# A four-layer gated network with cross attention on one core: where softmax sums and reciprocals are issued, when x comes back from DRAM, and which small loads stand in blocks of their own

## The reference, cut to what matters

```
q, k, v = proj(x), proj(ctx), proj(ctx)
p = exp(q k^T * scale - row maximum)        # layer 1: clipped to +-50, masked, no maximum
out = (p v) / p.sum(-1)
```

## Time and profile before

| | |
|---|---|
| time, median of 3 runs | 3059.93 us (3059.43 to 3064.61) |
| the profiled execution | 3059.54 us, span 3057.8 us |
| PE busy | 2632.1 us (86%) |
| PEld | 1671.9 us (55%) |
| DVE | 1753.8 us (57%) |
| ACT | 1196.7 us (39%) |
| POOL | 930.9 us (30%) |
| layer 1 attention starts | 549 us (its mask block 546) |
| layer 2 attention | starts 1537 us, first scores 1624.8 us |
| layer 3 attention | starts 2207 us, first scores 2276.8 us |

### The profile page before, as it was taken

How to read it: one execution, slowest core, us unless ns; L and a number is a source line. 1 busy time by engine, 2 the same in 40 slices (tenths; PEclk the granted TensorE clock), 3 DMA queues, 4 the chain that set the end, 5 groups by cost and what they waited for, 6 DMA issues and landing times. The chain is left out here.

```text
span 3057.8 us, 36158 instructions
## 1 busy us (share of the span) xinstructions
PE 2632.1 (86%) x11447; PEld 1671.9 (55%) x11447; DVE 1753.8 (57%) x3263; ACT 1196.7 (39%) x2550; POOL 930.9 (30%) x434
## 2 busy tenths in 40 slices
PE   7998799788887679999959998738699998699898
PEld 3555487655434456656546553426476653477555
DVE  2444576467765989989377664512277773444221
ACT  0222222267743688788014555111125553222111
POOL 0222000066732110010015775033318982322122
PEclk9998899899988889999979999869899999799999
DMA  9663113665403410100063421074465430212722
GB/s 278 223 241 139 55 62 124 182 166 142 111 1 114 165 56 28 46 37 28 14 170 107 132 68 29 1 288 110 106 183 172 121 102 1 84 41 71 262 56 47
DMA packets 137548, 333.52 MB, mean 109 GB/s; under 512 B 18608, under 2 KB 21681, under 8 KB 133041
## 3 DMA queue, kind: packets, MB, share of 16 engines
q1 hardware_dynamic: 110192, 262.71, 27.7%
q0 software_dynamic: 12864, 29.06, 4.1%
q10 hardware_dynamic: 14336, 39.85, 3.9%
HBM read 237.24 MB, written 97.72 MB: 110 GB/s over the span
## 5 line engine op out<-in xcount | busy, mean ns | idle before, releaser
L1982 POOL TENSOR_TENSOR L_attn_total<-L_attn_total,L_attn_probs 128x2048 f32<-128x2048 f32 x103 | 471.8, 4581 | 31.6 <-ACT L_attn_probs L1910 22.1
L2016 DVE TENSOR_REDUCE L_attn_row_max<-L_attn_rows_ps 128x1 f32<-128x512 f32 x512 | 338.9, 684 | 149.6 <-PE L_attn_rows_ps L1776 145.5
L1910 ACT ACTIVATE L_attn_probs<-L_attn_s_ps 128x512 f32<-128x512 f32 x512 | 288.0, 601 | 269.1 <-PE L_attn_s_ps L1797 264.2
L521 PE MATMUL L_ffn_hidden<-L_ffn_x_high,L_ffn_up_high 128*128 128x512 f32 x688 | 295.9, 430 | 73.2 <-DVE L_ffn_routes L432 25.8
L1797 PE MATMUL L_attn_s_ps<-L_attn_q_stack,L_attn_k_stack 98*128 98x512 f32 (+1 forms) x768 | 311.7, 432 | 21.1 <-ACT L_attn_probs L1910 20.7
L398 ACT ACTIVATE L_ffn_sums<-sims 128x128 f32<-128x128 f32 x1024 | 314.5, 389 | 29.0 <-DVE L_ffn_routes L418 22.3
L521 PE MATMUL L_ffn_hidden<-L_ffn_x_low,L_ffn_up_high 128*128 128x512 f32 x688 | 272.8, 397 | 0.0
L1776 PE MATMUL L_attn_rows_ps<-L_attn_k_stack,L_attn_q_stack 96*128 96x512 f32 x512 | 223.1, 439 | 23.0 <-DVE L_attn_row_max L2016 17.1
L542 PE MATMUL L_ffn_y<-L_ffn_down_in,L_ffn_h 128*128 128x512 f32 x512 | 230.8, 596 | 1.9 <-DVE L_ffn_h L649 1.9
L1797 PEld LDWEIGHTS L_attn_s_ps<-L_attn_q_stack,L_attn_k_stack 98*128 98x128 f32 (+1 forms) x768 | 145.7, 194 | 158.1 <-ACT L_attn_probs L1910 73.3
L1910 ACT ACTIVATE L_attn_probs<-L_attn_s_ps,keep_mask 128x512 f32<-128x512 f32 x256 | 183.8, 783 | 82.8 <-DVE L_attn_s_ps L2028 82.4
(11 more groups left out here) (310 smaller groups left out, 4526.2 us busy)
## 6 DMA issues: line engine op xcount, KB each, us to landing
L_attn_k_stack<-k_parts SPq DMA_DIRECT2D x144, 256.0 KB, 4.8
L_attn_q_stack<-q_parts SPq DMA_DIRECT2D x72, 256.0 KB, 6.0
k_parts<-L_attn_stage SPq DMA_DIRECT2D x32, 512.0 KB, 2.8
L_attn_abs_in<-in_L_ffn_w SPq DMA_DIRECT2D x12, 1024.0 KB, 10.8
L_attn_kv_parts<-L_attn_part ACTq DMA_DIRECT2D x12, 1024.0 KB, 4.8
L_attn_ctx<-ctx_parts SPq DMA_DIRECT2D x24, 512.0 KB, 9.3
L_attn_wv<-L_attn_kv_parts SPq DMA_DIRECT2D x24, 512.0 KB, 7.1
q_parts<-L_attn_stage SPq DMA_DIRECT2D x24, 512.0 KB, 3.6
```

Source lines behind the costliest of these rows:

```text
L521: last = nc.tensor.matmul(hidden_ps[0:m, b, side, :], w[:, i, e0:e0 + m], x_parts[xp][:, i, h * HALF:(h + 1) * HALF], start=(q == 0), stop ...
L1910: nc.scalar.activation(probs[:, g % P_SLOTS, h, :], s_ps[:, v % S_SLOTS, :], ACT.Exp, **kinds).then_inc(exp_done, 1)
L1982: nc.gpsimd.tensor_tensor(total[:], first, probs[:, g % P_SLOTS], ALU.add).then_inc(added, 1)
L2016: nc.vector.tensor_reduce(row_max[:, hq, i:i + 1], rows_ps[:, r % R_SLOTS, :], AX_X, ALU.max, negate=True).then_inc(max_done, 1)
```

## The change

- The output weights of layer 0 are loaded into the tiles of its value weights, from SP's list of the block before; its output block waits for nothing of its own.
- `key_mask_block` goes. The attention loads the mask first and VectorE converts it there.
- The biases are loaded ahead of the query weights in all three softmax attentions.
- `ffn_block` sets `tile_stats.taken` again after the work that runs in its beginning, so layer 2's attention uses the statistics taken at the end of layer 1.
- Layer 2's attention: DIRECT 2 for 1, sums at unit 2, reciprocals in eight parts of 64 columns at units 3, 3, 4, 4, 10, 10, 10, 10, and another opening.
- `routed_block` no longer loads x; layer 3's attention does, and takes the statistics at the new word S0 of its own opening. In the other openings S0 is the first word.

```diff
@@ ffn_block
             env.prefix = name
+            env.tile_stats.taken = final
@@ routed_block, sync
                 sp.wait_ge(summed, 16 * I)
-                if not last:
-                    for t in range(TILES):
-                        sp.dma_start(env.x[:, t, :], sums[t * P:(t + 1) * P, :]).then_inc(back[t], 16)
@@ routed_block, vector
                 copy_y(I - 1)
-                if not last:
-                    for t in range(TILES):
-                        dve.wait_ge(back[t], 16)
-                        env.tile_stats.take(env, dve, t)
-                    env.tile_stats.finish(dve)
@@ streamed_attention_block
-    DIRECT = {n: int(made or n == SETS - 2) if less_max_rows else 3 if n == SETS - 2 else 2 for n in range(SETS - 1)}
+    DIRECT = {n: 2 if made else int(n == SETS - 2) if less_max_rows else 3 if n == SETS - 2 else 2 for n in range(SETS - 1)}
...
-    SUMS_AT = 7 if less_max_rows else PV_AT
-    INVERT_AT = {u: part for part, u in enumerate((8, 9, 10, 11) if less_max_rows else (4, 6, 7, 8, 9, 10, 11, 12))}
-    INVERTED = SEQ // len(INVERT_AT)
+    SUMS_AT = 7 if less_max_rows and not made else PV_AT
+    invert_units = (3, 3, 4, 4, 10, 10, 10, 10) if made else (8, 9, 10, 11) if less_max_rows else (4, 6, 7, 8, 9, 10, 11, 12)
+    INVERT_PARTS = len(invert_units)
+    INVERT_AT = {u: [part for part, v in enumerate(invert_units) if v == u] for u in invert_units}
+    INVERTED = SEQ // INVERT_PARTS
...
     if made:
-        order = ("N0 X0 X1 N2 W0 W1 X2 X3 N4 Q00 V00 V01 X4 X5 W2 W3 N6 Q01 V02 V03 X6 X7 Q02 Q03 Q10 Q11 T0 Q12 Q13")
+        order = ("W0 W1 N0 N2 X0 X1 X2 X3 N4 Q00 W2 Q01 W3 V00 Q02 V01 N6 Q03 X4 X5 V02 X6 X7 V03 Q10 Q11 T0 Q12 Q13")
...
     else:
         order = ("N0 N1 K00 N2 N3 X0 X1 K01 N4 N5 X2 X3 W0 W1 V00 N6 N7 X4 X5 Q00 W2 W3 V01 X6 X7 Q01 K10 K11 "
                  "V02 V03 Q02 Q03 Q10 Q11 T0 Q12 Q13")
+    if x_sums is None:
+        order = "S0 " + order
+    else:
+        order = ("K00 K01 V00 V01 V02 S0 N0 N1 V03 X0 X1 W0 W1 N2 N3 X2 X3 Q00 N4 N5 W2 W3 Q01 X4 X5 N6 N7 K10 Q02 X6 X7 K11 "
+                 "Q03 Q10 Q11 T0 Q12 Q13")
@@ streamed_attention_block, sync
+                if not less_max_rows:
+                    sp.dma_start(mask_raw[:], io["mask"]).then_inc(mask_loaded, 16)
+                parts.load_biases(env, sp)
+                if x_sums is not None:
+                    for t in range(TILES):
+                        sp.dma_start(env.x[:, t, :], x_sums[t * P:(t + 1) * P, :]).then_inc(x_back[t], 16)
                 parts.first_loads(env, sp)
@@ streamed_attention_block, vector
+                def statistics():
+                    if not taken_before:
+                        for t in range(TILES):
+                            if x_sums is not None:
+                                dve.wait_ge(x_back[t], 16)
+                            nc.vector.bn_stats(stats[:, t, :], env.x[:, t, :]).then_inc(stats_done, 1)
...
@@ linear_attention_block, sync
+                sp.wait_ge(v_done, CT)
+                sp.dma_start(wv[:], wo_dram).then_inc(env.wo_loaded, 16)
+                sp.dma_start(bv[:], io["bo"].partition_broadcast(P)).then_inc(env.wo_loaded, 16)
```

More of the change, by code:

```diff
@@ L917, in _, with routed_block @@
                 dve.sem_inc(slots.placed, 1)
-def routed_block(env, name, slots, weights, load_weights, E, sums, last, ahead=None):
+def routed_block(env, name, slots, weights, load_weights, E, sums, ahead=None):
     nc = env.nc
@@ L934, in routed_block @@
     kept, summed, weighed = env.sem("kept"), env.sem("summed"), env.sem("weighed")
-    back = [env.sem(f"back{n}") for n in range(TILES)]
     weight_step = env.sem("weight_step")
@@ L1582, in streamed_attention_block @@
     env.wo_loaded = env.sem("wo_loaded")
+    x_back = [env.sem(f"x_back{t}") for t in range(TILES)] if x_sums is not None else []
     with ExitStack() as local:
@@ L1848, in _ @@
                         turn(0)
-                    elif item[0] not in "WN":
+                    elif item[0] not in "WNS":
                         for c in range(DC):
@@ L2521, in sb @@
             return local.enter_context(nc.sbuf_tensor(f"{name}_{n}", shape, dt))
-        if early:
+        if weights:
+            wo, bo = weights
+        elif early:
             wo, out_rows = env.out_weights[:, 0], env.out_weights[:, 1]
@@ L2758, in x_hat, with expert_layer @@
                 yield
-        def expert_layer(name, gate, shared, normalise, sums, last=False, ahead=None):
+        def expert_layer(name, gate, shared, normalise, sums, ahead=None):
             with sublayer() as local:
@@ L2890, in build @@
             expert_layer("L3_ffn", env.tanh_gates[:, 7:8], io["L3_ffn_shared_w1"].shape[0], False,
[L2891 removed]
+                         out.rearrange("b s d -> (b s) d"))
         else:
```

100 lines of the change are left out of this document (47 added, 53 removed).

## The result

The changed kernel took 3076.81 us (median of 5, 3076.05 to 3082.73), the kernel before 3059.93 beside it: ratio 1.0059, 95% interval 1.0045 to 1.0073. Forecast was 3064, +4.8 on the profiled execution; the profiled execution is 16.7 longer (span 3074.5 against 3057.8).

What follows compares the result with a forecast made beforehand. TensorE, busy 2632 of 3058 us, was taken as the bound. Terms -5.3 - 2.9 - 4.8 + 9.8 + 8.0 = +4.8 on the profiled 3059.54 gave 3064 us, range 3047 to 3077.

Steps and rivals of the forecast that it cites:

- C and D: Opening of layer 2's attention: kept statistics and the new order together save time, -4.8 us (-1 to -9).
- E: Layer 2's attention sets: third addend, earlier sums and reciprocals in eight parts cost +9.8 us.
- F: Layer 3's attention: x reloaded inside it and the new opening order cost +8.0 us (-6 to +12).
- A: Layer 0's output block: loading its weights early removes TensorE's wait, -5.3 us (-4.8 to -6.5).
- B: Before layer 1's attention: dropping the mask block and loading biases earlier saves -2.9 us (-2.4 to -3.4).
- Q00 starts at 23, -4.2: Layer 2's opening: first query product starts 23 us after the attention's start, 4.2 us earlier than before.
- about 1 less: Layer 2's opening: TensorE's 4.42 us wait behind N6 shrinks by about 1 us, since GpSimd's subtractions come earlier.
- I take the same loss: Layer 2's sets: slow clock costs as much as before, some 7.9 us over five sets.
- only one half of keys is left beside it, so I take 10.7: Layer 3's opening: first query product's end to first row takes 10.7 us, against 13.2 before.
- With the 1.3 of a block border the attention starts at 2197.35, 9.9 before: Border into layer 3: attention starts 1.3 us after the last sum lands, 9.9 us earlier than before.
- rival B2: Layer 3's opening: TensorE finds no costly hole, the 9.9 us arrive whole, 3046 us; chance 0.15.
- B3: Layer 2's sets: the clock loses more, making them cost +20 us, 3074 us in all; chance 0.20.

Runs made afterwards that it cites:

- best1: Changed kernel with E undone, layer 3's old order, x loads issued at routed block's end, awaited in attention, no GpSimd drain there: 3046.84 us, ratio 0.9959.
- A to D alone: Changed kernel with E and F both undone: 3051.16 us, ratio 0.9978 to the kernel before.
- E_late_inv: Changed kernel with layer 2's reciprocals in four parts of 128 columns at units 8 to 11, sums still at unit 2: 3065.37 us, ratio 1.0027.

## Why the prediction was wrong

The sign of every part was right; the sum was 12 us too low. Of these, 2.1 are in C and D, 0.3 in E, 3.7 in F's border, 1.5 in F's opening and 4.2 in layer 3's sets.

**A, B** came as worked out (-5.2 and -2.6 for -5.3 and -2.9).

**C and D**: the step "Q00 starts at 23, -4.2" held (22.8), and so did N0 hit by the subtraction. The step that failed is "about 1 less" of the 4.42 wait behind N6. It became 5.56, with 1.18 for Q00's stacked parts in front: with Q00 4 us earlier and N6 behind V01, the rows run into N6 sooner and meet all of it. N6 itself did get shorter (5.2 us from its start, 7.1 before). I took away the subtraction and didn't ask what an earlier row does to a wait that VectorE's order sets. +2.1 of the miss. This is read from the two timelines; no run varies it.

**E**: right in sum (+10.1 in the ledger), with terms off in both directions. The addend was 0.95 a set (0.93), the waits for maxima +0.5 (I had 1.0), and the slow clock, which I took as unchanged, went from 7.3 to 11.3 over sets 1 to 5 (PE busy beyond 34.04 before, beyond 34.99 after). So "I take the same loss" is the step that failed, by 4.0, and the five sets cost 11.3 for 9.5. Set 0, which has no sums of a set before it, was 1.5 shorter by its clock, set 6 1.8 longer, and set 7's end gave 1.5. That these errors cancel is luck: the second traces of the two kernels have 315.0 against 297.1 for the same stretch, +17.9. What the experiments add is where the price sits: not in the addend, which I charged with 0.9 a set, but in the eight reciprocals ahead of or among the maxima.

**F** was the real miss, +17.5 with layer 3's sets against +8.0. Its opening looks right, 81.5 from start to T0 for my 80.0, 4.43 in front of X0 for my 4.5, but two errors in it nearly cancel. Q00 starts at 31.8 and not 33.8. Against that it takes 5.5, at 1.2 GHz, for 4.7, and the step "only one half of keys is left beside it, so I take 10.7" failed: from Q00's end to the first row it is 12.9, as in the kernel before (13.0), and the wait there is 7.22 for 5.9.

Two other steps failed. "With the 1.3 of a block border the attention starts at 2197.35, 9.9 before": only 6.2. The 1.3 was read where VectorE came last; with its statistics gone, GpSimd's drain after the last scatter is the last at that border, 6.2 from the end of its issue to the next block, and without it the start moves by 3.7, as shown. So the time freed was cut by the next engine in line, and rival B2's gain could not have been 9.9 with the drain in place.

The other is that layer 3's sets cost nothing: they cost 4.2. It is not settled whose these are. F isn't needed for them, since the kernel without F has 4.7 there. T0 to T7 of layer 3 takes 260.7 to 260.9 in three traces (both of before, and best1, which has A to D), 262.7 to 262.9 in five, and 264.3 to 265.8 in ten; A to D alone is in the second group and in the third. So some 2 us of it change from one execution of a kernel to the next, and the changed kernel was at the high end twice. The clock behind T0's wait is 1.5 of them: set 0 takes 37.9 to 38.1 at 0.96 in twelve traces and 36.4 to 36.5 at 1.00 in six. That some kernels meet it more often is only seen.

B3 came nearest in time (3074), but for other reasons than its own: the clock in E lost 4 more, not 10. The median lies 0.2 us below the upper end of my range, and that it lies inside is luck: the upper end stands for B3, a slow clock that makes E cost 20, and that didn't happen; 0.42 for slower was too little, since F's gain was read from a row that doesn't price it.

Why the clock comes down with eight reciprocals (units 3 and 4, 6 and 7, or spread) and not with four at units 8 to 11 and the sums at unit 2, though TensorE idles 1.9 to 2.8 us a set in each, stays open. Four at units 8 to 11 alone don't keep it up: with the sums at unit 7 it falls in three of the sets 1 to 5 with three addends, and in three to five of them, by trace, with two. That the waits stand close together, my theory, isn't refuted by the spread kernel, whose waits still do; but it can't be the whole answer, since the same two waits come with a fall in every set of the kernel without E, with none in one set of the first trace of before, and with none at all in E_late_inv. That they stand early was hardly varied by the kernel with units 6 and 7, whose waits came 0.9 us later. No kernel had four parts at early units, or eight at late ones alone.

Two slips of reading moved nothing: the value bias is there 5.63 behind its issue (556.20 less 550.57) and not 5.65, and the slow stretch shown as 1674.9 to 1680.4 runs from 1673.9 to 1680.7.
